# A fused recurrent and windowed-attention kernel: the linear gate moved from the odd to the even iterations

## What is computed

```
# branch s: linear attention, 16 heads of 32, per-head decay for the first 8
v, p = split(ln(xn) @ W_in);  q = ln(xn) @ Wq + bq;  k = ln(xn) @ Wk + bk
q, k = softmax over each head's 32;  k = (1-smear)*k + smear*k_of_the_row_before
attn = tril(q k^T * decay);  o = attn / (row sum + eps) @ v
s = ln(silu(p) * o @ W_out)
# branch f: two layers of windowed attention (8 heads of 64, window 128, own and
# previous window) and a gated MLP (682 hidden)
x = x + attention(l2norm(q), l2norm(k), rotated) @ wo
x = x + (a * gelu(g)) @ w2 + b2,   with a, g = ln(shifted x) @ w1 + b1
```

## Time and profile before

| | |
|---|---|
| median of three executions | 2001.72 us (1994.23 to 2002.28) |
| the profiled execution, its own time | 1996.89 us |
| its span, first to last instruction | 1995.1 us |
| TensorE busy, share of the span | 1906.7 us, 96% |
| VectorE | 1728.3 us, 87% |
| ScalarE | 1196.3 us, 60% |
| GpSimd | 1021.3 us, 51% |
| granted TensorE clock, mean | 0.993 |
| DMA, mean | 36 GB/s |

### The profile page before, as it was taken

The page is one execution under the profiler, slowest core; times in us unless marked ns, Lnnn a source line. Parts: engine busy times, 40 slices in busy tenths (PEclk is TensorE's granted clock), DMA queues, the critical chain, the costliest instruction groups (busy, mean ns, idle before and its releaser), DMA issues.

```text
span 1995.1 us, 48979 instructions
## 1 busy us (share of the span) xinstructions
PE 1906.7 (96%) x15178; PEld 1635.3 (82%) x15178; DVE 1728.3 (87%) x5308; ACT 1196.3 (60%) x2862; POOL 1021.3 (51%) x1004
## 2 busy tenths in 40 slices
PE   5899999999999999999999999999999999999998
PEld 3787888888888888888788888888888888888887
DVE  5888888988889888888877998888998888998886
ACT  3565655656556656566565665665665665666564
POOL 2554555645456554555534555545555545554542
PEclk8999999999999999999999999999999999999999
DMA  5010000000000100001102111111111101111101
GB/s 197 20 33 27 24 25 25 27 29 21 26 26 24 32 20 25 29 21 32 64 28 75 36 41 37 32 29 42 32 42 34 32 29 42 32 42 34 33 27 37
DMA packets 81152, 72.76 MB, mean 36 GB/s; under 512 B 13484, under 2 KB 74344, under 8 KB 81096
## 3 DMA queue, kind: packets, MB, share of 16 engines
q1 hardware_dynamic: 81096, 72.05, 11.8%
HBM read 42.64 MB, written 16.78 MB: 30 GB/s over the span
## 4 chain that ended last, share of the span: by engine, by line
PE 56%; DVE 20%; issue 14%; ACT 6%; POOL 2%; DVEq 1%; SPq 0%; POOLq 0%; ACTq 0%; DMA 0%
PE bank L1502 34%; PE bank L1507 11%; PE bank L1514 8%; PE bank L1549 3%; ACT L939 2%; DVE sq_sum L1294 2%; DVE prob L1041 2%; ACT gel L939 1%; DVE prob L1060 1%; DVE rot L1397 1%; DVE state L1093 1%; ACT mix_work L929 1%; DVE kT L1232 1%; DVE mix_work L1362 1%; DVE mix_work L1349 1%
## 5 line engine op out<-in xcount | busy, mean ns | idle before, releaser
L1502 PE MATMUL bank<-hT_n,w_s 128*128 128x128 f32 x3072 | 402.9, 281 | 22.9 <-ACT gel L939 22.0
L1502 PEld LDWEIGHTS bank<-hT_n,w_s 128*128 128x128 f32 x3072 | 364.7, 191 | 54.8 <-ACT gel L939 29.4
L823 ACT ACTIVATE prob<-prob,row_min 128x256 f32<-128x256 f32 x512 | 256.9, 505 | 168.1 <-DVE row_min L1041 167.7
L1507 PE MATMUL bank<-wqkv_s,xT 128*128 128x512 f32 x1152 | 320.1, 413 | 6.2 <-DVE wqkv_s L1214 3.4
L705 POOL TENSOR_TENSOR rot_other<-raw,rot_t 128x256 f32<-128x256 f32 x256 | 188.9, 769 | 221.8 <-ACT raw L792 221.8
L663 POOL TENSOR_TENSOR inv_norm<-sq_clip,half_neg 128x8 f32<-128x8 f32 x128 | 261.0, 2047 | 75.2 <-DVE sq_clip L1297 75.1
L1507 PEld LDWEIGHTS bank<-wqkv_s,xT 128*128 128x128 f32 x1152 | 208.2, 192 | 54.7 <-DVE wqkv_s L1214 5.4
L1041 DVE CUSTOM_DVE_ANT_0 prob<-bank,table,inv_norm 128x256 f32<-128x256 f32 x512 | 226.2, 478 | 3.4 <-issue 3.1
L1502 PE MATMUL bank<-w_s,hid 128*128 128x256 f32 x768 | 200.9, 385 | 0.0
L792 ACT ACTIVATE pT<-bank 128x512 f32<-128x512 f32 x256 | 140.2, 609 | 48.5 <-PE bank L1514 48.4
L1060 DVE TENSOR_SCALAR prob<-prob,row_inv 128x256 f32<-128x256 f32 x448 | 145.4, 367 | 8.0
(11 more groups left out here) (180 smaller groups left out, 4268.8 us busy)
## 6 DMA issues: line engine op xcount, KB each, us to landing
k_prev<-k_carry SPq DMA_DIRECT2D x32, 224.0 KB, 2.5
x_s<-in_L_attn_x SPq DMA_DIRECT2D x32, 128.0 KB, 2.1
rot_s<-in_rotary SPq DMA_DIRECT2D x64, 64.0 KB, 2.0
rows_normalised<-xh SPq DMA_DIRECT2D x32, 128.0 KB, 1.7
y_n<-rows_normalised SPq DMA_DIRECT2D x32, 128.0 KB, 2.2
x_between_layers<-x SPq DMA_DIRECT2D x32, 128.0 KB, 1.7
s_between_passes<-s_out SPq DMA_DIRECT2D x32, 128.0 KB, 1.7
x_s<-x_between_layers SPq DMA_DIRECT2D x32, 128.0 KB, 2.1
```

The source lines that it names most:

```text
L823: ins = act.activation(prob[:, h, :], prob[:, h, :], ACT.Exp, bias=row_min[:, c:c + 1], scale=-1.0, accum_out=row_sum[:, c:c + 1])
L1502: return pe.matmul(out, lhsT, rhs, start=first, stop=last)
L1507: ins = pe.matmul(out, halved(left[:, a]), halved(right[:, b]), start=first and n == 0, stop=last and n == 2)
```

## The change

- The gate `p` of a chunk is projected, evicted, put through tanh and multiplied in the even iteration (`two`) and no longer in the odd one. Its two tiles were parts of `mix_work`; now p goes to `gate`, and the tangent to `k_carry`, the tile of the keys that are shifted, so the tangent waits for the three transfers out of it. `mix_read` no longer multiplies by the gate; one product over 512 columns (`gate_read`) does it later in the even iteration.
- TensorE projects the local values ahead of the second group of hidden products, in all iterations.
- VectorE makes the low half of the turned keys (`low_turned(u, "kt", ...)`) ahead of the first norm's steps and of half of the state's sum. The norm's variance (`norm2_var`) moves into the next iteration, after the weighting of a0, and its root on GpSimd with it. The sum of the queries' exponentials goes behind the low half and the third scaling of scores. In the even iteration the first scaling of scores goes behind `scores("a0")`.
- In the odd iterations the weighting of a1 moves from VectorE to ScalarE, ahead of the copy of the local keys.

The diff without its context and without the lists of step names, the unchanged steps that only change their place, and the helper `weigh` of ScalarE (which is `weigh_b0` with the step as an argument):

```diff
@@ -248,2 +247,0 @@
-        p_lin = mix_work[:, 2 * ME:3 * ME]
-        p_tanh = mix_work[:, 3 * ME:4 * ME]
@@ -262,0 +261,2 @@
+
+        gate_tanh = k_carry[:, :]
...
@@ -683,0 +684,2 @@
+                if 1 <= i.low < NW:
+                    norm2(proj)
@@ -731,2 +732,0 @@
-                    if one is None:
-                        root(inv_norm[:, p, 0:H], sq_clip[:, 0:H], H).then_inc(proj_pool.done("invq"), 1)
@@ -735,4 +734,0 @@
-                    pool.wait_ge(mix_act.sem, mix_act.at("tanh", n))
-                    pool.tensor_tensor(gate[:, :], p_tanh, p_lin, ALU.mult).then_inc(mix_pool.done("gatep"), 1)
-                    pool.wait_ge(mix_pool.sem, mix_pool.at("gatep", n))
-                    pool.tensor_tensor(gate[:, :], gate[:, :], p_lin, ALU.add).then_inc(mix_pool.done("gate"), 1)
@@ -744,0 +741,7 @@
+                if two is not None:
+                    pool.wait_ge(mix_act.sem, mix_act.at("tanh", two))
+                    pool.tensor_tensor(gate_tanh, gate_tanh, gate[:, :], ALU.mult).then_inc(mix_pool.done("gatep"), 1)
+                    pool.wait_ge(mix_pool.sem, mix_pool.at("gatep", two))
+                    pool.tensor_tensor(gate[:, :], gate_tanh, gate[:, :], ALU.add).then_inc(mix_pool.done("gate"), 1)
+                if proj is not None and one is None:
+                    root(inv_norm[:, proj.parity, 0:H], sq_clip[:, 0:H], H).then_inc(proj_pool.done("invq"), 1)
@@ -760,2 +762,0 @@
-                if i.low + 1 < NW:
-                    norm2(i.back(-1))
...
@@ -894,0 +896,2 @@
+                    if one is not None:
+                        weigh("a1", a)
...
@@ -925,3 +928,5 @@
-                if one is not None:
-                    act.wait_ge(mix_dve.sem, mix_dve.at("p", one))
-                    act.activation(p_tanh, p_lin, ACT.Tanh, scale=0.5).then_inc(mix_act.done("tanh"), 1)
+                if two is not None:
+                    act.wait_ge(mix_dve.sem, mix_dve.at("p", two))
+                    act.wait_ge(k_shifted, 48 * (two.number() + 1))
+                    act.activation(gate_tanh, gate[:, :], ACT.Tanh, scale=0.5).then_inc(mix_act.done("tanh"), 1)
+                if one is not None:
@@ -1015,0 +1021,2 @@
...
@@ -1081,3 +1088,6 @@
-                dve.wait_ge(mix_dve.sem, mix_dve.at("o" + k, mix))
-                dve.tensor_tensor(go[:, cols], go[:, cols], gate[:, cols], ALU.mult)\
-                   .then_inc(mix_dve.done("go" + k), 1)
+
+            def gate_read(mix):
+
+                dve.wait_ge(mix_pool.sem, mix_pool.at("gate", mix))
+                dve.wait_ge(mix_dve.sem, mix_dve.at("o1", mix))
+                dve.tensor_tensor(go[:, :], go[:, :], gate[:, :], ALU.mult).then_inc(mix_dve.done("go"), 1)
...
@@ -1311,2 +1321,0 @@
-                if two is not None:
-                    decay_scores(two, 0)
@@ -1325,0 +1335 @@
+                    decay_scores(two, 0)
@@ -1338,0 +1349,5 @@
+                if 1 <= i.low < NW:
+                    norm2_var(u)
+                if a is not None:
+                    if one is not None:
+                        inverse("a1", a)
@@ -1343 +1358,7 @@
-                if a is not None:
+                if two is not None:
+                    dve.wait_ge(mix_pe.sem, mix_pe.at("p", two))
+                    dve.tensor_tensor(gate[:, :], mix_bank[1][:, :], bias_mix[:, 1, :], ALU.add)\
+                       .then_inc(mix_dve.done("p"), 1)
+                if a is not None and one is not None:
+                    inverse("b0", a)
+                if a is not None and one is None:
@@ -1345,2 +1365,0 @@
-                    if one is not None:
-                        inverse("b0", a)
@@ -1361,3 +1379,0 @@
-                    dve.wait_ge(mix_pe.sem, mix_pe.at("p", one))
-                    dve.tensor_tensor(p_lin, mix_bank[1][:, :], bias_mix[:, 1, :], ALU.add)\
-                       .then_inc(mix_dve.done("p"), 1)
@@ -1432,0 +1449,2 @@
+                if two is not None:
+                    gate_read(two)
@@ -1440,0 +1459,22 @@
+                if two is not None and i.low < UNITS:
+                    state_add(two, 0)
...
+                if a is not None:
+                    residual(a, att_bank[1])
...
+                if u is not None:
+                    low_turned(u, "kt", "kl", kT[:, :, :, u.parity, :], proj_bank)
+                if nxt is not None:
+                    norm2(nxt)
+                if two is not None and i.low < UNITS:
+                    state_add(two, 2)
...
+                if one is not None:
+
+                    decay_scores(one, 2)
@@ -1446,23 +1485,0 @@
-                if two is not None and i.low < UNITS:
-                    state_add(two, 0)
-                    state_add(two, 2)
...
-                if a is not None:
-                    residual(a, att_bank[1])
...
-                if nxt is not None:
-                    norm2(nxt)
-                if u is not None:
-                    low_turned(u, "kt", "kl", kT[:, :, :, u.parity, :], proj_bank)
...
-                if one is not None:
-
-                    dve.wait_ge(mix_pool.sem, mix_pool.at("gate", one))
-                    decay_scores(one, 2)
-                    decay_scores(one, 3)
@@ -1470,0 +1488,2 @@
+                if one is not None:
+                    decay_scores(one, 3)
...
@@ -1729,0 +1749,3 @@
+
+                    pe.wait_ge(mix_dve.sem, mix_dve.at("s1", two))
+                    mix_linear(two, "p", mix_bank[1], win_s, ME)
@@ -1752,0 +1775 @@
+                    pe.wait_ge(mix_dve.sem, mix_dve.at("p", two))
@@ -1756,3 +1778,0 @@
-                if one is not None:
-                    pe.wait_ge(mix_dve.sem, mix_dve.at("k", one))
-                    mix_linear(one, "p", mix_bank[1], win_s, ME)
@@ -1771,0 +1792,3 @@
+                if u is not None:
+                    pe.wait_ge(proj_act.sem, proj_act.at("k", u))
+                    proj_linear(u, "v", 2 * E)
@@ -1775,3 +1797,0 @@
-                if u is not None:
-                    pe.wait_ge(proj_act.sem, proj_act.at("k", u))
-                    proj_linear(u, "v", 2 * E)
@@ -1801 +1821 @@
-                    pe.wait_ge(mix_dve.sem, mix_dve.at("p", one))
+                    pe.wait_ge(mix_dve.sem, mix_dve.at("k", one))
@@ -1819 +1839 @@
-                    pe.wait_ge(mix_dve.sem, mix_dve.at("go1", two))
+                    pe.wait_ge(mix_dve.sem, mix_dve.at("go", two))
```

42 lines of the change are left out of this document (22 added, 20 removed).

## The result

| | before | after |
|---|---|---|
| median of the runs (6 each) | 1997.97 us (1992.53 to 2002.28) | 1983.33 us (1975.71 to 1983.95) |
| ratio of the runs, 95% interval | | 0.9908, 0.9885 to 0.9930 |
| span of the profiled execution | 1995.1 us | 1981.6 us |

The change makes the kernel 0.9% faster (0.7 to 1.15% by the interval).

What follows compares the result with a forecast made beforehand. TensorE was taken to bound the iteration pair, with VectorE close. Layer 0 -28 and +8, layer 1 -8 and +22, drain +1.5, together -4 us from 1996.9 to 1993, plus half the distance to the median: 1995 us, range 1966 to 2014.

Steps and rivals of the forecast that it cites:

- Gate's projection, +1.5 in the even iteration: TensorE: six products leave the odd iteration for the even one, priced in full at +1.5 us; own waits 0 to 0.1.
- Low half, -0.95 in every iteration of layer 0, -0.1 in layer 1's even one: VectorE makes the keys' low half earlier, so TensorE's wait goes: -0.95 us per layer 0 iteration, -0.1 in layer 1's even.
- part 6 of the prediction: Gate products on GpSimd, state's decay, tangent, gelu and DMA: moving them costs nothing on the path.
- Values' projection covers gelu, up to -0.7: TensorE, odd iterations: the projection's 1.6 us cover the 0.71 us wait for gelu, up to -0.7 us.
- the fourth step: Odd iterations: the key sum limits the gain; layer 0's turning of mixed keys comes 0.44 + 0.4 = 0.8 us earlier.
- Layer 1, -0.5 by the port: Layer 1's odd iterations: VectorE's two-input SBUF steps stand until GpSimd's subtraction ends, so turning comes only 0.5 us earlier.
- with 0.43 us less of key sum: Odd iterations: if the key sum gains 0.43 us less than said, 10 us slower; it comes later than now.
- all of it is recovered: Rival, 0.27: key sum keeps ahead of TensorE, odd iterations gain 2.2 + 0.95 and 2.2 us; 1943 us, half 1968.
- Gains nothing: Rival, 0.17: the key chain gains nothing or loses, odd iterations give only 0.95 in layer 0; 2014 us.
- still waited for: Rival, 0.06: TensorE still waits for the keys' low half, so the 0.95 terms fall away; 2024 us.

Runs made afterwards that it cites:

- a_kl_back: Changed kernel with the keys' low half back at its old place on VectorE, behind the norm's product and state sum; 2001.0 us, ratio to before 1.0007.
- a_v_back: Changed kernel with the values' projection back behind the second hidden group; 1982.3 us, ratio to before 0.9921.
- a_turn: Changed kernel with mixed queries and attention queries turned ahead of the mixed keys, on TensorE and in ScalarE's copies; 1977.7 us, ratio to before 0.9901.
- a_root_back: Changed kernel with the root of the norm's variance back behind the rotation table on GpSimd; 1986.0 us, ratio to before 0.9953.
- a_cos: Changed kernel with the rotation's first product on VectorE ahead of attention's first low half; 1963.9 us, ratio to before 0.9833.
- a_p_switch: Changed kernel with the gate's projection behind the keys' projection in the first iteration of layer 1 alone; 1984.4 us, ratio to before 0.9922.
- a_weigh_back: Changed kernel with the weighting of a1 in odd iterations back from ScalarE to VectorE; 1974.6 us, ratio to before 0.9874.
- b_kl: Kernel before, with only the keys' low half moved up on VectorE as in the change; 1984.8 us, ratio to before 0.9944.
- a_clip_tt: Changed kernel with the floor of the squared norms taken by a two-tensor form instead of tensor and number; 1977.7 us, ratio to before 0.9901.
- b_kl_v: Kernel before, with only the keys' low half moved up and the values' projection ahead of the second hidden group; 1986.9 us, ratio to before 0.9956.

## Why the prediction was right or wrong

1. *Gate's projection, +1.5 in the even iteration.* Right. With the low half's own value taken out (a_kl_back), the even iterations grew by 0.53 + 1.08 = 1.61 and 1.24 + 0.28 = 1.52. New waits in them: none.
2. *Low half, -0.95 in every iteration of layer 0, -0.1 in layer 1's even one.* The size held, the cause only by half. In both iterations of layer 0 the wait went: in the odd one 0.95 of the 2.14 us lie behind the turning of the mixed keys. But in the changed kernel the move itself is worth 1.08 in the even and nothing in the odd iteration, and 0.28 in layer 1's even one (a_kl_back). In the odd one the gate's second product on GpSimd had made the keys' norm on VectorE take 1.70 instead of 0.68 us; with it in the even iteration, and the variance's two steps gone, the low half is in time at either place (read from rows, a_kl_back). I had put those products at nothing (part 6 of the prediction).
3. *Values' projection covers gelu, up to -0.7.* Right as a cover, and the fourth step cut it down rightly: 0.23 in layer 0 and nothing in layer 1 (a_v_back).
4. *The key sum ends last in the odd iteration, so only what it gains counts.* The mechanism held: the new wait is there 32 times, 0.71 in layer 0 and 1.06 in layer 1 (forecast 0.8 to 1.2), the distance of sum and key sum stayed (5.87 and 5.89), the exponential starts at the subtraction's end, and a change at another place (a_turn, a_v_back) moved a wait and little else. The size was off: 1.2 us earlier in layer 0, not 0.8. The cause is my "nothing" for the root's move on GpSimd, 0.43 (a_root_back, where the turning comes 0.78 earlier). It is the step that failed in layer 0: I had asked who waits for that root, and not whose instruction the table behind it had been standing beside.
5. *Layer 1, -0.5 by the port.* -0.57. The first product of the finish does start when the subtraction is over (1565.03 against 1565.08). What stood until then is the clip of 16 columns ahead of it in the queue, which reads one tile in SBUF, so this place does not show a rule on two inputs; nor did the clip's 0.52 us in the earlier trace rows, which I had taken to speak for it. a_cos does show it. The Trainium skill ("SBUF — State Buffer", section "Who interferes with whom") has two-input steps in SBUF and GpSimd's reads exclude each other, and a_cos shows both directions of it (GpSimd's product 1.91 instead of 1.05 us, VectorE's 1.73 instead of 1.23). Rule and runs agree, and without the rule I would have forecast 1.0.
6. *The rest, nothing.* No new wait came from the tangent and the state's decay. Wrong for the gate's products, whose leaving the odd iterations is worth the 1.0 us on VectorE of point 2. Wrong, too, for what lies outside the steady loop, where I put nothing at all. At the switch the gate's projection stands ahead of the projection that waits for cut weights, and covers 1.4 us of that wait and a fall of the clock (a_p_switch: 2.6 us of the 6.5). The first five iterations took 2 us more instead of 4 less; how much of that is the change, one execution does not tell.

The sum, then: the path was right, and two causes were missing in it. One, the root, made layer 0's odd iterations 0.4 us better. The other, the gate's products on GpSimd with the variance's steps, did there what I had credited to the low half, so the sum did not notice. That part is luck, and so is it that the first five iterations (6 us above the forecast) made up for most of the switch (6.5 below). One reading in the prediction is wrong as well: with 0.43 us less of key sum the turning would still come 0.4 and 0.1 us earlier than before, not later. The weighting on ScalarE, which I priced as part of step 4, costs 0.43 us per odd iteration in layer 1 and 0.07 in layer 0 (a_weigh_back); the change would be better without it.

Of the rivals, "all of it is recovered" had 1943 to 1968 us, 15 and more below the result, and its mechanism (VectorE's load decides) was shown false: more load on VectorE (a_weigh_back) made the kernel faster. "Gains nothing" and "still waited for" did not come.

## What to carry to other kernels

When an engine's wait is covered by work moved ahead of it, look for what that engine needs next: here the wait for gelu went and 0.23 of 0.7 us stayed. The same move may be worth 1 us in one iteration and 0 in the next, so undo each part alone in the changed kernel before it is credited. A product taken off GpSimd can shorten a VectorE instruction beside it, here from 1.70 to 0.68 us. And look at the iterations outside the steady loop: nearly half of this gain was at the switch of the layers, where a covered wait also kept the clock up, and in the steady iterations one part (b_kl) does better than the whole change.

## What the runs showed of the hardware that was not expected

*A wait of about 2 us can cost more than itself.* The changed kernel's fifth iteration took 31.86 us and its neighbours of the same kind 28.91. VectorE's key sum waited there for the transfer of the shifted keys:

```profile
187.74 0.69 DVE L1431 TENSOR_TENSOR mix_work<-mix_work,k_prev 128x512 f32<-128x512 f32 x1 [1.26 <-DMA k_prev<-k_carry]
```

and TensorE for the key sum, 2.06 instead of 0.71 us:

```profile
188.56 0.65 PE L1533 MATMUL bank<-table,mix_work 128*128 128x128 f32 x4 [2.06 <-DVE mix_work L1431]
...
190.17 1.91 PE L1521 MATMUL bank<-w_s,hid 128*128 128x256 f32 x4
```

```profile
184.00:188.50 4.50, 2.35 (x26) 1.83 (x24) 3.20 (x4) 1.69 (x5) 2.72 (x2) 1.00 0.22 61
188.50:192.00 3.50, 3.44 (x17) 3.08 (x18) 3.42 (x12) 1.68 (x3) 1.17 (x2) 0.67 0.01 3
```

Behind that wait the mean granted clock was 0.67 over 3.5 us (0.50, the lower of its two levels, from 189.7 to 193.0, and full behind that), and a group of four products that takes 1.13 us took 1.91. Of the 2.95 us lost, 1.35 are the longer wait and the rest is the clock. In a_clip_tt the same wait was 1.94 us, the clock stayed at 1.00, and the iteration took 30.14:

```profile
187.13 0.65 PE L1536 MATMUL bank<-table,mix_work 128*128 128x128 f32 x4 [1.94 <-DVE mix_work L1434]
```

A fall stands beside a wait at the switch, too (2.30 us of wait and 0.66 before; 1.64 and 0.82 in a_p_switch; 0.23 and 1.00 after). Waits of 0.7 to 1.1 us in the steady loop left the clock at 1.00. The length of the wait alone does not decide: behind 1.86 us the clock fell in a_weigh_back (at 128.1), behind 2.16 us in a_v_back (at 1026.5) and 3.46 us in b_kl_v (at 1040.6) it stayed at 1.00. What does was not tested. A wait of 0.7 us in every odd iteration does make the one behind a late transfer longer; whether that makes the spread of the runs (1975.7 to 1983.9 us) was not shown, since only one execution of each kernel has a profile.

*A small VectorE step can stand for a whole GpSimd instruction, whatever its form.* The floor on 128x16 elements took 1.19 us in layer 0 and 1.95 in layer 1 beside GpSimd's subtraction, in both forms; alone it takes 0.17. The norm of the hidden rows took 0.76 instead of 0.35 beside a GpSimd product of 0.75, and the keys' norm 1.70 instead of 0.68 beside one of 1.27. The second was on the path in layer 0, and so, before the change, was the third.
